# Linear attention: outputs computed feature by feature instead of token by token, denominators from a scan of the keys folded into the gate

## The reference, cut to what matters

```
b, t, d = x.shape
q = _phi((x @ W_Q.T).reshape(b, t, H, DK))      # phi(u) = elu(u) + 1
k = _phi((x @ W_K.T).reshape(b, t, H, DK))
v = (x @ W_V.T).reshape(b, t, H, DK)
gamma = jax.nn.sigmoid(decay_log)               # one decay for each head
def step(carry, inp):
    S, z = carry
    qt, kt, vt = inp
    S = g4 * S + jnp.einsum('bhi,bhj->bhij', kt, vt)
    z = g3 * z + kt
    num = jnp.einsum('bhij,bhi->bhj', S, qt)
    den = jnp.sum(z * qt, axis=-1, keepdims=True) + EPS
    return ((S, z), num / den)
...
gate = jax.nn.sigmoid(x @ W_g_w.T + W_g_b).reshape(b, t, H, DK)
y = (outputs * gate).reshape(b, t, H * DK)
return y @ W_O.T
```

## Time and profile before

| | us |
|---|---|
| three runs, median (lowest to highest) | 1907.86 (1907.04 to 1908.34) |
| profiled execution, its own time | 1906.6 |
| its span, first to last instruction | 1904.8 |
| PE busy | 1877.7 (99%) |
| DVE busy | 1255.5 (66%) |
| ACT busy | 880.7 (46%) |
| POOL busy | 574.6 (30%) |

### The profile page before, as it was taken

The page is one execution under the profiler, slowest core; times in us unless marked ns, Lnnn a source line. Parts: engine busy times, 40 slices in busy tenths (PEclk is TensorE's granted clock), DMA queues, the critical chain, the costliest instruction groups (busy, mean ns, idle before and its releaser), DMA issues.

```text
span 1904.8 us, 36309 instructions
## 1 busy us (share of the span) xinstructions
PE 1877.7 (99%) x12353; PEld 1625.4 (85%) x12353; DVE 1255.5 (66%) x2807; ACT 880.7 (46%) x1716; POOL 574.6 (30%) x523
## 2 busy tenths in 40 slices
PE   8999999999999999999999999999999999999998
PEld 7888888888788888888888888888888888788887
DVE  6566566656768888765555555565666556888885
ACT  6756656665654444443333333333333332444443
POOL 6313202320331223133433333333333333522211
PEclk9999999999999999999999999999999999999999
DMA  7100000000032211220000000000000001122322
GB/s 244 42 1 0 0 0 0 0 0 0 13 77 33 30 29 29 34 66 12 12 10 11 8 9 8 11 11 11 11 11 11 12 12 23 32 62 62 65 55 57
DMA packets 230630, 53.19 MB, mean 28 GB/s; under 512 B 209696, under 2 KB 228768, under 8 KB 230176
## 3 DMA queue, kind: packets, MB, share of 16 engines
q1 hardware_dynamic: 229296, 49.53, 12.9%
q10 hardware_dynamic: 1264, 2.76, 0.4%
HBM read 18.69 MB, written 8.39 MB: 14 GB/s over the span
## 4 chain that ended last, share of the span: by engine, by line
PE 88%; POOL 4%; DVE 2%; issue 2%; SPq 1%; DMA 1%; ACT 1%; ACTq 0%; DVEq 0%; POOLq 0%
PE PS L323 18%; PE PS L1200 16%; PE PS L1209 9%; PE PS L332 7%; PE PS L858 7%; PE PS L829 6%; PE PS L1661 5%; PE PS L1704 4%; PE PS L1647 4%; PE PS L847 3%; PE PS L1668 2%; PE PS L1681 2%; PE PS L869 2%; SPq L271 1%; PE PS L1693 1%
## 5 line engine op out<-in xcount | busy, mean ns | idle before, releaser
L323 PE MATMUL PS<-ln_xh,lin_w 128*128 128x512 f32 x768 | 250.1, 394 | 4.9 <-DVE lin_state L1522 4.7
L1132 ACT ACTIVATE ff_silu<-PS 128x512 f32<-128x512 f32 x192 | 114.1, 595 | 235.3 <-PE PS L1200 207.0
L1167 DVE SCALAR_TENSOR_TENSOR ff_h<-PS,ff_silu 128x512 f32<-128x512 f32 x192 | 131.2, 684 | 110.2 <-PE PS L1200 96.3
L1436 ACT ACTIVATE lin_yg_hi<-stage 128x512 fp32r<-128x512 f32 x64 | 40.4, 632 | 317.8 <-DVE stage L1531 167.4
L323 PEld LDWEIGHTS PS<-ln_xh,lin_w 128*128 128x128 f32 x768 | 144.2, 188 | 36.2 <-issue 7.4
L565 POOL TENSOR_TENSOR qk<-qk,swapped 64x128 f32<-64x128 f32 (+2 forms) x96 | 96.8, 1008 | 239.6 <-DVE swapped L709 233.8
L1151 DVE TENSOR_TENSOR ff_h_lo<-ff_h,ff_h_hi 128x512 fp32r<-128x512 f32 x192 | 164.5, 857 | 0.4
L858 PE MATMUL PS<-probT,v_a 128*128 128x128 f32 x1152 | 153.3, 278 | 0.0
L858 PEld LDWEIGHTS PS<-probT,v_a 128*128 128x128 f32 x1152 | 139.5, 192 | 14.3 <-issue 7.3
L1493 DVE TENSOR_TENSOR lin_AD<-PS,lin_decay 128x512 f32<-128x512 f32 x128 | 82.0, 682 | 104.6 <-PE PS L1647 104.6
L323 PE MATMUL PS<-ln_xl,lin_w 128*128 128x512 f32 x384 | 150.0, 391 | 0.0
(11 more groups left out here) (177 smaller groups left out, 5301.8 us busy)
## 6 DMA issues: line engine op xcount, KB each, us to landing
ff_raw<-ln_xn SPq DMA_DIRECT2D x464, 32.0 KB, 2.0
ln_xl<-ln_xn SPq DMA_DIRECT2D x288, 32.0 KB, 2.0
out_x<-X SPq DMA_DIRECT2D x15, 512.0 KB, 2.9
X<-in_x SPq DMA_DIRECT2D x7, 1024.0 KB, 5.5
stage<-in_w_lin SPq DMA_DIRECT2D x1, 2048.0 KB, 8.2
stage<-in_w_gate SPq DMA_DIRECT2D x2, 768.0 KB, 7.4
stage<-in_w_up SPq DMA_DIRECT2D x2, 768.0 KB, 8.9
stage<-in_w_down SPq DMA_DIRECT2D x2, 768.0 KB, 10.2
```

What stands on the lines that cost most here:

```text
L323: last = nc.tensor.matmul(out, w, x, start=n == 0, stop=n == len(terms) - 1)
L1132: nc.scalar.activation(silu[:, f % NB_GU, :], PS[:, f % NB_GU, :], ACT.Silu, scale=W_SCALE).then_inc(silu_done.sem, 1)
L1167: nc.vector.scalar_tensor_tensor(h[:, f % 2, :], PS[:, NB_GU + f % NB_GU, :], W_SCALE, silu[:, f % NB_GU, :], ALU.mult, ALU.mult).then_inc ...
```

## The change: what it does

**Outputs.** The values of a head (128 keys by 64 features) are now fixed in the array and the decayed scores are streamed, 128 tokens at a time. The two heads of a pair use the two column halves of the array and write partitions 0 to 63 and 64 to 127 of the same bank. The state is fixed and the decayed queries are streamed. The result has features on the partitions at once, so that `quotient`, `transposed_output` and the column of ones are gone, and `gated` is a plain product of the bank and `gate`.

**Denominators.** They are made for a whole half. DVE scans the keys along the tokens, z = gamma z + k (`key_sums`, four scans of 128x512, the first behind item 3, the other three behind item 7). POOL multiplies each by the queries (`sums_by_query`), each behind its `qsT`, which now waits for the scan as well; in a batch's first half it also copies the scan's last column. PE adds the features of each head with a matrix of zeros and ones (`denominators`, four matmuls with 32 columns of weights and 512 streamed) into bank 7. DVE adds the constant and takes the reciprocal of 128x512 (`inverse`). PE spreads each head's row over 64 partitions (`spread`, eight matmuls with 32 rows and 64 columns of weights and 512 streamed) into four banks, and DVE multiplies (1 + tanh) by them (`gate_scale`, four instructions of 128x512).

**Banks.** `keys` always uses bank 6, the state bank 4 alone, outputs banks 2 and 3 in turn; the waits of items 0 to 3 of a half change with them.

```diff
-        RING = (5, 2, 3, 4)
-        ST_BANK = (4, 5)
+        RING = (5, 2, 4, 3)
+        KEY_BANK, OUT_BANK, ST_BANK, DEN_BANK = 6, (2, 3), 4, 7
+        SPREAD_BANK = (6, 5, 7, 3)
...
                     for j in range(NP):
-                        pool.wait_ge(phi_done.sem, phi_done.at(b, 2 * NP * half + 2 * j + 1))
+                        pool.wait_ge(z_done.sem, z_done.at(b, NP * half + j + 1))
                         nc.gpsimd.tensor_tensor(qsT[:, j, :].rearrange("p (c t) -> p c t", t=P),
...
+                        sums_by_query(b, half, j)
...
+            def sums_by_query(b, half, j):
+
+                if half == 0:
+                    nc.gpsimd.tensor_scalar(z_last[:, j:j + 1], z[j][:, UN - 1:UN], 1.0, None, ALU.mult).then_inc(z_kept.sem, 1)
+                    pool.wait_ge(z_kept.sem, z_kept.at(b, j + 1))
+                nc.gpsimd.tensor_tensor(z[j], z[j], qT[:, j, :], ALU.mult).then_inc(zq_done.sem, 1)
...
-            def quotient(b, c, g):
...
+            def key_sums(b, half, j):
+
+                dve.wait_ge(phi_done.sem, phi_done.at(b, 2 * NP * half + 2 * j + 2))
+                nc.vector.tensor_tensor_scan(z[j], decay[:, j:j + 1].to_broadcast([P, UN]), kT[:, j, :],
+                                             0.0 if half == 0 else z_last[:, j:j + 1], ALU.mult, ALU.add).then_inc(z_done.sem, 1)
+
+            def inverse(b, half):
+
+                dve.wait_ge(den_ready.sem, den_ready.at(b, half + 1))
+                nc.vector.tensor_scalar(den, PS[:, DEN_BANK, :], DEN_EPS, 2.0, ALU.add, ALU.mult).then_inc(den_done.sem, 1)
+                dve.wait_ge(den_done.sem, den_done.at(b, half + 1))
+                nc.vector.reciprocal(den, den).then_inc(inv_done.sem, 1)
+
+            def gate_scale(b, half):
+                dve.wait_ge(gate_done.sem, gate_done.at(b, NP * (half + 1)))
+                dve.wait_ge(spread_ready.sem, spread_ready.at(b, half + 1))
+                for j in range(NP):
+                    nc.vector.scalar_tensor_tensor(gate[:, j, :], gate[:, j, :], 1.0, PS[:, SPREAD_BANK[j], :],
+                                                   ALU.add, ALU.mult).then_inc(scale_done.sem, 1)
...
                     for it in range(2 * NP):
                         phi_item(b, half, it)
-                        if rest and it == 0:
-                            gated(b, c0 - 1)
+                        if it == 2 * NP - 1:
+                            for j in range(1, NP):
+                                key_sums(b, half, j)
+                        elif it == 3:
+                            key_sums(b, half, 0)
...
                     scaled_keys(b, c0)
+                    inverse(b, half)
                     nln.dve_normalise(dve, nturn)
...
-                        for g in range(2):
-                            quotient(b, ch, g)
+                        if c == 0:
+                            gate_scale(b, half)
+                            nfront.dve_blocks(dve, nturn, (front, b * NHALF + half))
...
+            def denominators(b, half):
+
+                pe.wait_ge(zq_done.sem, zq_done.at(b, NP * (half + 1)))
+                pe.wait_ge(x_done.sem, x_done.at(b, UT * half))
+                for j in range(NP):
+                    last = nc.tensor.matmul(PS[j * SUM:(j + 1) * SUM, DEN_BANK, :], head_sum[:], z[j], start=True, stop=True)
+                last.then_inc(den_ready.sem, 1)
+
+            def spread(b, half):
+
+                pe.wait_ge(inv_done.sem, inv_done.at(b, half + 1))
+                pe.wait_ge(v_done.sem, v_done.at(b, UT * (half + 1)))
+                pe.wait_ge(ks_done.sem, ks_done.at(b, UT * half + 1))
+                for j in range(NP):
+                    rows = slice(j * SUM, (j + 1) * SUM)
+                    for r in range(2):
+                        row = j * SUM + r * SUM // 2
+                        last = nc.tensor.matmul(PS[r * DK:(r + 1) * DK, SPREAD_BANK[j], :],
+                                                ident[rows, row:row + 1].to_broadcast([SUM, DK]), den[rows, :],
+                                                start=True, stop=True)
+                last.then_inc(spread_ready.sem, 1)
...
-                for hh in range(HG):
-                    last = nc.tensor.matmul(bank[:, hh * VA:(hh + 1) * VA], AD[:, ch % 2, hh % 2, 2 * g + hh // 2, :], v[:, c, HG * g + hh, :],
-                                            start=hh == 0, stop=ch == 0, skip_group_check=True)
...
+                pe.wait_ge(yg_done.sem, yg_done.at(b, ch - 1))
+                for j in range(NP):
+                    for r in range(2):
+                        last = nc.tensor.matmul(bank[r * DK:(r + 1) * DK, j * P:(j + 1) * P], v[:, c, 2 * j + r, :],
+                                                AD[:, ch % 2, r, j, :], start=j == 0, stop=ch == 0, skip_group_check=True)
...
-                for j in range(NP):
-                    last = nc.tensor.transpose(PS[:, 6, j * P:(j + 1) * P], y[:, ch % 2, j * P:(j + 1) * P], ident[:])
...
                             keys(b, half, 0)
+                            if first and half == 0:
+                                pe.wait_ge(zeroed, 5)
+                            denominators(b, half)
```

More of the change, by code:

```diff
@@ L1444, in turn @@
                             decay_tables()
-                        if first and half == 0 and it == 3 * NP:
-                            act.wait_ge(zeroed, 2)
                         m = NITEM * half + it
@@ L1663, in outputs @@
-                if ch > 0:
-                    if g == 0:
-                        pe.wait_ge(s_done.sem, s_done.at(b, ch))
-                    for jj in range(2):
-                        j = 2 * g + jj
-                        last = nc.tensor.matmul(bank[:, jj * 2 * VA:(jj + 1) * 2 * VA], qsT[:, j, c * P:(c + 1) * P],
-                                                S[:, j, :], start=False, stop=True, skip_group_check=True)
+                if c == 1:
+                    pe.wait_ge(scale_done.sem, scale_done.at(b, NP * (half + 1)))
@@ new lines, in outputs @@
+                pe.wait_ge(yg_done.sem, yg_done.at(b, ch - 1))
+                for j in range(NP):
+                    for r in range(2):
+                        last = nc.tensor.matmul(bank[r * DK:(r + 1) * DK, j * P:(j + 1) * P], v[:, c, 2 * j + r, :],
+                                                AD[:, ch % 2, r, j, :], start=j == 0, stop=ch == 0, skip_group_check=True)
+                if ch > 0:
+                    pe.wait_ge(s_done.sem, s_done.at(b, ch))
+                    for j in range(NP):
+                        last = nc.tensor.matmul(bank[:, j * P:(j + 1) * P], S[:, j, :], qsT[:, j, c * P:(c + 1) * P],
+                                                start=False, stop=True, skip_group_check=True)
@@ L1670, in outputs, with state @@
                 last.then_inc(o_ready.sem, 1)
[L1672 removed]
+            def state(b, half, c):
                 ch = UT * half + c
[L1674 to L1677 removed]
+                pe.wait_ge(ks_done.sem, ks_done.at(b, ch + 1))
+                if ch == 0:
                     pe.wait_ge(s_done.sem, s_done.at(b, 0))
[L1679 to L1681 removed]
+                for j in range(NP):
+                    last = nc.tensor.matmul(PS[:, ST_BANK, j * P:(j + 1) * P],
@@ L1717, in turn @@
                         projection(b, half, it)
-                        if rest and it == 1:
-                            transposed_output(b, c0 - 1, False)
                         if rest and it in (2, 5):
@@ L1734, in turn @@
                             pe.wait_ge(qs_done.sem, qs_done.at(b, NP * (half + 1)))
-                        if c + 1 < UT:
-                            for g in range(2):
-                                outputs(b, half, c, g)
-                                state(b, half, c, g)
-                        else:
-                            outputs(b, half, c, 0)
-                            if ch + 1 < NC:
-                                keys(b, half, c)
-                            outputs(b, half, c, 1)
-                            if ch + 1 < NC:
-                                for g in range(2):
-                                    state(b, half, c, g)
-                        if c >= 1:
-                            transposed_output(b, ch - 1)
-                        if c >= 2 and not (last and ch == TB - 1):
+                            spread(b, half)
+                        outputs(b, half, c)
+                        if c == UT - 1 and ch + 1 < NC:
+                            keys(b, half, c)
+                        if ch + 1 < NC:
+                            state(b, half, c)
+                        if c >= 2:
                             out_projection(b, ch - 2)
```

146 lines of the change are left out of this document (57 added, 89 removed).

## The result

| | before | after |
|---|---|---|
| median of the runs beside each other, us | 1907.45 | 2064.82 |
| lowest to highest | 1907.0 to 1908.34 | 2064.47 to 2069.75 |
| profiled span | 1904.8 | 2063.1 |
| mean granted clock | 0.997 | 0.962 |

The changed kernel is slower: the ratio is 1.083, 95% interval 1.081 to 1.085. The forecast was 1998 with a range of 1930 to 2070. So sign and range held, and 67 of the 157 us that were lost were not forecast.

What follows compares the result with a forecast made beforehand. PE, busy 99% of the span, was taken to bound the kernel. Per half, -2.0 own work, +5.4 pause, +1.7 clock and +0.55 other waits gave +5.65, +90 us over 16 halves: 1998 us, range 1930 to 2070.

Steps and rivals of the forecast that it cites:

- PE's own work: PE's matmuls and transposes in a half of linear attention, with changes of array shape: -2.0 us a half.
- the pause ahead of `denominators`: PE stands still behind `keys` of chunk 0 until POOL's four products are done: 5.4 us a half, bounds 4.1 and 7.5.
- the clock: PE's granted clock falls to 0.50 after the pause, costing 1.7 us a half, bounds 0 and 3.4.
- all other waits of PE: Waits for scaled keys and state, less the bank wait that goes: net +0.55 us a half.
- stays under PE's time and costs only in the places named: DVE loses eight quotient groups a half, gains scans, reciprocal and scalings, and delays PE only at the waits listed.
- The reciprocal: In `inverse` on DVE: 9.7 ns an element, some 5.1 us for 512, covered by PE's values and `scores`.
- State behind `keys` in chunk 3: In a batch's first half PE waits 1.0 us for the scaled keys before the state's matmuls.
- Bank wait ahead of item 0: The 0.58 us wait for the state in eight halves goes, as item 0 uses a free bank: -0.3 a half.
- Rival 1: The wait ahead of `denominators` comes but the clock holds: 1971 us; chance 0.18.
- Rival 2: Scans and products are hidden, done within 4.85 us of the phi: 1885; faster if within 6.3; chance 0.11.
- Rival 3: POOL's chain is at its shortest and the clock holds: 1946 us, chance 0.08; all upper bounds give 2065.
- Rival 4: Column parts of the array don't overlap in outputs, `denominators` and `spread`: 7.0 us a half more, 2110; chance 0.11.

Runs made afterwards that it cites:

- experiment 3: Changed kernel with each key scan directly behind its own pair's phi and the block transpose back ahead of the chunks; 1897.99 us, ratio 0.995 to the kernel before.
- experiment 6: experiment 3 with the outputs' head loops exchanged, four heads of one column half first, then four of the other; 1924.47 us, ratio 1.010 to the kernel before.
- experiment 2: Changed kernel with only the next half's block transpose back behind the normalisation, ahead of the chunks; 2009.92 us, ratio 1.054 to the kernel before.
- experiment 5: Changed kernel with six useless float32 matmuls of 128x512 on PE ahead of its wait for POOL's products; 2035.52 us, ratio 1.069 to the kernel before.

## Why the prediction was right, and where it fell short

- **The whole, by terms.** Against the forecast PE's own work came out 2.8 lower, the pause ahead of `denominators` 10.8 higher, the clock 21.6 higher and all other waits of PE 38.3 higher (W_O 41.2, the rest -2.9): 68 together, by the profiled spans. The result lies 5 us inside the upper end of the range. That end stood there for the unknown sizes of the terms that the forecast had; a wait that it did not have filled the room, so that the range held is luck in good part.
- **PE's own work.** Forecast -2.0 a half, -32; measured -34.8. The outputs take 1.02 a chunk with the change of shape in it, forecast 0.88 and some 0.2. `denominators` takes 1.06 for its 8 rows in the chain of experiment 3, at full clock, `spread` 1.05 for 16: the 0.86 and 0.2 of the forecast. What the prediction drew from the Trainium skill, "TensorE: Matmul & The Clock Gate", Part 3, is that matmuls in different column groups run at the same time. The traces agree, by these rows and by experiment 6.
- **The pause ahead of `denominators`.** Forecast 5.4 for each half, 86; measured 97.2, 6.22 in first halves, 5.44 in second ones, and 10.2 once. Three of its terms were off, by little. A scan takes 1.22 to 1.28 where nothing holds it up, not 1.0; that is 1.8 times the 0.69 of the like-sized DVE instruction and nearer to the upper bound of 1.38. The Trainium skill's "DVE: opcode table, instruction layouts, handler registers and perf-mode slots", Datapath and trigger behaviour, has the scan at half throughput, and by these rows that roughly holds. The scans hold POOL up by some 1.8 and not by 1.0. And the copy of the last column, taken as 0.3, takes 1.1 beside a scan.
- **The step that failed** is the sentence that DVE "stays under PE's time and costs only in the places named". The block transpose was listed in DVE's queue, behind the gate's scalings, and I followed it only to PE's next wait for DVE. I did not follow it through SP's moves to ACT, where the copy of the moved data stands in front of `gated_high`. No term stood for that: 41.2 us of idle time at W_O, which experiment 2 takes away but for 2.2.
- **The clock.** Forecast 1.7 a half, 27; measured 48.8. Behind the first pause it is 2.1 a half, 33.8, and filling that pause gave back 1.8 (experiment 5), so that term was near. The rest is mostly the fall behind the second pause, 16.7, the same omission. The 41.2 and the 16.7 together are most of the 67 us between forecast and result.
- **The reciprocal.** Forecast 5.1 for 128x512 from short rows; it takes 3.35 (median 3353 ns), 6.5 ns an element. It was covered in either case.
- **Small waits.** State behind `keys` in chunk 3: forecast 1.0 eight times, measured 6.3 in eight. State in chunk 1, 0.7 forecast: not seen. Bank wait ahead of item 0: forecast to go; it went. In front of L322 there is now a wait for POOL's `ln_xl`, 6.3 in 11; with the block transpose back it is still 5.1 (experiment 2) and 5.0 (experiment 3).
- **Rivals.** Rival 1, the clock holds: wrong. Rival 2, faster because the chain is hidden: wrong here, but its condition was the right one, and experiment 3 shows what lies behind it. Rival 3's upper end, 2065, meets the result by numbers and not by its mechanism. Rival 4, no overlap of column parts: wrong, by PE's rows and by experiment 6.

## What to carry to other kernels

When an instruction is moved on one engine, follow what it starts through every queue to the end: here DVE to SP to ACT to POOL to PE, and the 41 us were lost on ACT, behind a copy that had nothing to do with the step that waited. A matmul that waits for a long chain of another engine belongs behind so much other work that the chain is done when its engine gets there, and the chain's source goes directly behind its input; together with the block transpose back in its place and `keys` ahead of the outputs, that made a change that cost 157 us into one that gains 24. On this kernel a pause of 5.4 us or more cost its length and some 2 us of clock, pauses of 1.5 to 4 us cost clock too where the level fell behind them, and with two pauses in a half most of the clock's loss went only when both were gone.

## What the runs showed of the hardware

- DVE's scan and POOL's products hold each other up. Scans of second halves, and the reciprocal, in the whole span of the changed kernel; shortest, median and longest in ns:

```profile
L1512 DVE TENSOR_TENSOR_SCAN lin_zq<-lin_tmp_a,lin_z_last,lin_kT x16: 1273/1276/1277, 885.8 to 1731.0; 128x512 f32<-128x512 f32 x16
L1512 DVE TENSOR_TENSOR_SCAN lin_AD<-lin_tmp_a,lin_z_last,lin_kT x16: 1255/1751/2248, 893.9 to 1733.3; 128x512 f32<-128x512 f32 x16
...
L1520 DVE RECIPROCAL lin_zq<-lin_zq x16: 3352/3353/3354, 846.7 to 1744.3; 128x512 f32<-128x512 f32 x16
```

The first line's scans run while POOL does nothing of the kind. Those of the second run beside POOL's `qsT` and product: one of each two takes 1.26, the other 2.25, and POOL's 1.26 becomes 2.18. They take turns, each waiting for the end of the one before it, as the times under the first pause show.
- Doing more on PE can take less time: 12 useless rows in a half, and the kernel was 29 us faster. They filled waiting time (86.5 us less of it for 83.0 of work), and the clock's loss fell by 28.8.
- Column parts of the array overlap even where the partner stands four rows back in the queue: 0.49 us lost in a chunk and not 0.88. Rows written later can start ahead of rows written earlier for another part (experiment 6).
- A reciprocal of 512 elements takes 6.5 ns an element; the rows of one and four elements (149 and 178 ns) gave 9.7.
